# Attention in a transformer layer kernel: maxima of the first three key groups from the split keys in 32-row products, and a reordered end

## The reference, cut to what matters

```python
x = x + xattn(layernorm(x), ctx)          # 16 heads of 32, keys = values = ctx (4 x 2048 x 512)
    scores = einsum('bthd,bshd->bhts', q * s, k * s); w = softmax(scores); out = (w @ v) @ w_proj.T + b_proj
x = x + gated_scan_block(layernorm(x))    # rmsnorm, W_in -> u, z, g; tanh, sigmoid; scan over 128 tokens; W_out
x = x + moe(layernorm(x))                 # 8 experts of 512, top 2, and a shared expert of width 1024
```

## Time and profile before

| what | value |
|---|---|
| median of 3 runs | 531.94 us (531.33 to 532.11) |
| profiled execution, its own time | 533.81 us |
| its span | 532.0 us |
| PE busy | 472.7 us (89%) |
| DVE busy | 404.4 us (76%) |
| ACT busy | 327.2 us (61%) |
| POOL busy | 290.3 us (55%) |
| chain that ended last | PE 51%, DVE 27%, issue 8%, DMA 7%, ACT 3%, POOL 2% |

### The profile page before, as it was taken

The page is one execution under the profiler, slowest core; times in us unless marked ns, Lnnn a source line. Parts: engine busy times, 40 slices in busy tenths (PEclk is TensorE's granted clock), DMA queues, the critical chain, the costliest instruction groups (busy, mean ns, idle before and its releaser), DMA issues.

```text
span 532.0 us, 15785 instructions
## 1 busy us (share of the span) xinstructions
PE 472.7 (89%) x6731; PEld 330.7 (62%) x6731; DVE 404.4 (76%) x598; ACT 327.2 (61%) x362; POOL 290.3 (55%) x274
## 2 busy tenths in 40 slices
PE   0568888999999999999989945999999999999994
PEld 0135655676667767767666533844878788787642
DVE  3567576778877888787762798698599999999426
ACT  3336466766766787676654473456579888888320
POOL 1146499899999999999769430482001101010032
PEclk9999798999999999999999996999999999999998
DMA  6885789988899987897991830086999999997125
GB/s 203 243 225 170 188 228 269 241 240 236 240 254 266 262 257 208 222 261 185 362 403 56 297 121 37 1 270 220 420 358 419 417 418 417 416 417 328 41 80 177
DMA packets 29821, 133.97 MB, mean 252 GB/s; under 512 B 6452, under 2 KB 6708, under 8 KB 18996
## 3 DMA queue, kind: packets, MB, share of 16 engines
q1 hardware_dynamic: 25880, 120.38, 69.2%
q0 software_dynamic: 3680, 12.06, 6.2%
q10 hardware_dynamic: 192, 0.52, 0.5%
HBM read 96.77 MB, written 11.01 MB: 203 GB/s over the span
## 4 chain that ended last, share of the span: by engine, by line
PE 51%; DVE 27%; issue 8%; DMA 7%; ACT 3%; POOL 2%; SPq 1%; DVEq 0%; ACTq 0%; POOLq 0%
PE bank L1026 10%; PE bank L1061 10%; DVE ws L807 9%; PE bank L1046 8%; DVE mx L722 7%; PE bank L1070 6%; DMA wst<-in_ffw 5%; PE bank L1186 2%; PE bank L1187 2%; PE bank L1188 2%; DVE hf L948 1%; PE bank L1129 1%; POOL ps L638 1%; DVE hl L953 1%; DMA kstk<-kl 1%
## 5 line engine op out<-in xcount | busy, mean ns | idle before, releaser
L722 DVE TENSOR_REDUCE mx<-bank 128x1 f32<-128x512 f32 x240 | 154.7, 686 | 56.7 <-PE bank L1026 54.7
L638 POOL TENSOR_TENSOR ps<-pt 128x512 f32<-128x512 f32 x128 | 159.6, 1273 | 13.2 <-PE bank L1070 6.7
L477 ACT ACTIVATE pt<-bank 128x1024 f32<-128x1024 f32 x128 | 124.3, 1023 | 63.6 <-PE bank L1046 62.3
L807 DVE SCALAR_TENSOR_TENSOR ws<-wst,ws 128x2048 f16<-128x2048 f32 x51 | 115.5, 2283 | 1.8 <-ACT ws L525 1.2
L525 ACT ACTIVATE ws<-wst 128x2048 f16<-128x2048 f32 x48 | 90.7, 1905 | 6.1 <-DMA wst<-in_ffw 6.0
L613 POOL TENSOR_TENSOR kl<-kt,kh 128x512 f16<-128x512 f32 x58 | 67.6, 1186 | 27.3 <-ACT kh L442 27.2
L1201 PE MATMUL bank<-xt,ws 128*128 128x128 f16 x480 | 81.2, 219 | 0.5 <-DVE hf L948 0.5
L1202 PE MATMUL bank<-xt,ws 128*128 128x128 f16 x480 | 81.2, 219 | 0.0
L1203 PE MATMUL bank<-xt,ws 128*128 128x128 f16 x480 | 81.2, 219 | 0.0
L1026 PE MATMUL bank<-kstk,q 96*128 96x512 f16 x176 | 69.8, 423 | 10.2 <-DMA kstk<-kl 5.7
L679 POOL DMA_DIRECT2D ys_rows<-xn x15 | 8.2, 544 | 120.9 <-ACT xn L594 120.9
(11 more groups left out here) (170 smaller groups left out, 722.2 us busy)
## 6 DMA issues: line engine op xcount, KB each, us to landing
wst<-in_ffw SPq DMA_DIRECT2D x51, 1024.0 KB, 11.4
kt<-in_keysT SPq DMA_DIRECT2D x16, 1024.0 KB, 6.0
v<-in_vals SPq DMA_DIRECT2D x16, 1024.0 KB, 9.9
kstk<-kh SPq DMA_DIRECT2D x84, 128.0 KB, 4.0
kstk<-kl SPq DMA_DIRECT2D x44, 128.0 KB, 3.3
wst<-kh SPq DMA_DIRECT2D x40, 128.0 KB, 4.3
xs_rows<-biases SPq DMA_DIRECT2D x15, 256.0 KB, 3.0
x_tok<-xs_rows POOLq DMA_DIRECT2D x15, 256.0 KB, 7.9
```

The lines of the kernel that those rows point to most:

```text
L477: act.activation(pt[:, n % 4, :, :, :].rearrange("p j a t -> p (j a t)"), bank[:, 2 * (n % 2):2 * (n % 2) + 2, :].rearrange("p j n -> p (j ...
L638: pool.tensor_tensor(ps2[:, n % 4, :, :], pt[:, n % 4, 0, :, :], pt[:, n % 4, 1, :, :], ALU.add)\
L722: dve.tensor_reduce(mx[:, a, q:q + 1], bank[:, 4 + k % 2, :], AX.X, ALU.max).then_inc(m_taken, 1)
L807: dve.scalar_tensor_tensor(ws[:, home_of(q), 1, m, :, :].rearrange("p c n -> p (c n)"), wst[:, q % 2, m, :, :].rearrange("p c n -> p (c n) ...
```

## The change

- Groups 0, 1 and 2 (`ROWS = 3`) take their maxima without the stack. The queries are repeated over the four 32-row lanes and split into high and low (`zw`: ACT, then DVE for group 0 and POOL for 1 and 2), transposed by PE into `q0`, and `max_pair(j, k)` forms two blocks at a time, each as three accumulating matmuls of 32 rows by 512 columns (high by `kh`, low by `kh`, high by `kl`), the two blocks on neighbouring lanes and neighbouring banks. For groups 1 and 2 a pair waits until both banks are read.
- The start is reordered: the first norm and its queries before the key split, keys of group 1 loaded at once, the ones rows and three quarters of `x` later, the stack of group 0 behind. Statistics of batches 1 to 3 move from the start into body 1, with ACT's square root there.
- At the end, the constants load one body earlier, the first expert weights in bodies 13 and 14, POOL adds the bias in bodies 13 and 14, DVE takes the pair sums of the last group, `scale_win`, the small constants and `split_low(0, 0)` move into or right behind body 15. The residual sum `x1 + normed(x1)` becomes one DVE operation with row factors, so POOL has one addition a batch there, not two.

The diff, cut to its core:

```diff
+ROWS = 3
+    wide = wproj.bitcast(F16).rearrange("p n (a z c) -> p n a z c", a=HG, z=2)
+    zw, q0 = wide[:, 0:2, :, :, :], wide[:, 2:4, :, :, :]
...
@@ sync queue, start
+        load_k(1)
+        stack(0, 0)
+        load_k(2)
+        load_v(0)
...
-        sp.wait_ge(kt_in[0], 16)
-        sp.dma_start(x[:, 1:B, :], t["x"][:, 1:B, :]).then_inc(x_in, 16)
-        sp.wait_ge(split_hi, 2)
-        copies(0, 0, kh, (0, 2 * HD))
...
+        stack(0, 1)
         stack(1, 0)
-        load_k(2)
         stack(1, 1)
         load_k(3)
         load_v(1)
+        sp.dma_start(x[:, 1:B, :], t["x"][:, 1:B, :]).then_inc(x_in, 16)
...
+            if i == G - 4:
+                for dst, name in CONSTS:
+                    sp.dma_start(dst, t[name]).then_inc(consts, 16)
+            if i in (G - 3, G - 2):
+                for m in ((0,), (1, 2))[i - G + 3]:
+                    sp.dma_start(wst[:, 0, m, :, :], t["ffw"][0, m]).then_inc(w_in[0][m], 16)
@@ scalar
+        def wide_high(j):
+            q, _ = queries_of(j)
...
+            act.activation(zw[:, j % 2, :, 0, :].rearrange("p a (r d) -> p a r d", r=HG),
+                           q.unsqueeze(2).broadcast_to([P, HG, HG, HD]), ACT.Copy).then_inc(wide_hi, 1)
+        def take_wide(j):
...
+            for half in range(2):
+                act.activation(q0[:, j % 2, 2 * half:2 * half + 2, :, :].rearrange("k a z t -> k (a z t)"),
...
+        root(ln1_var, 1, 0, 1)
+        wide_high(0)
         for h in range(2):
             split_keys(0, h)
-        root(ln1_var, 1, 0, 1)
-        act.wait_ge(split_hi, 2)
-        stack_rows(act, 0, 1, kh, (0, 2 * HD))
...
+                if i == G - 2 and p == 1:
+                    split_first(0)
...
+                if i == 1 and p == 2:
+                    root(ln1_var, B, 1, B)
...
+        act.activation(r1[:, 0, 0:2], eps[:, :], ACT.Sigmoid)
@@ gpsimd
-        for i in range(G):
+        for i in range(G - 1):
             for hs in range(HS):
                 pair_sum(HS * i + hs)
...
+                if i in (G - 3, G - 2) and hs in (2, 5):
+                    add_bias(2 * (i - G + 3) + hs // 3)
-        add_bias()
...
         for b in range(B):
-            pool.wait_ge(h_done, b + 1)
-            pool.wait_ge(x1b_done, b + 1)
-            pool.tensor_tensor(x2[:, b, :], x2[:, b, :], xn[:, b, :], ALU.add).then_inc(x2p_done, 1)
+            pool.wait_ge(x1h_done, b + 1)
+            pool.tensor_tensor(x2[:, b, :], x2[:, b, :], bout[:, :], ALU.add).then_inc(x2p_done, 1)
@@ vector
+                if i == G - 1:
+                    for n in (HS * i + 2 * p, HS * i + 2 * p + 1):
+                        pair_sum(n)
...
+                if i == 1 and p < 3:
+                    dve.wait_ge(x_in, 16)
+                    first_norm(p + 1, p + 2)
...
+                if i == G - 1 and p == 0:
+                    scale_win()
+                if i == G - 1 and p == 1:
+                    make_constants()
...
+        split_low(0, 0)
...
+            dve.tensor_scalar(x2[:, b, :], x1[:, b, :], r1[:, 2, b:b + 1], r1[:, 1, b:b + 1], ALU.mult, ALU.add)\
+                .then_inc(x1h_done, 1)
-        dve.wait_ge(one_set, 2)
-        dve.tensor_scalar(starts[:, :], iota[:, :], float(P), None, ALU.mult)
...
-        split_low(0, 0)
@@ tensor
+        def max_pair(j, k):
+            a, q = block_of(k)
+            pe.wait_ge(wq_done, 2 * j + a // 2 + 1)
+            pe.wait_ge(split_hi, 2 * j + a // 2 + 1)
             if j > 0:
-                pe.wait_ge(m_taken, MB * j + k - 1)
-            elif k >= 6 and k % 2 == 0:
+                pe.wait_ge(m_taken, MB * j + k)
+            elif k >= 6:
                 pe.wait_ge(m_taken, k - 4)
...
+            home = 4 if j > 0 else k % 6
+            for n, (z, keys) in enumerate(((0, kh), (1, kh), (0, kl))):
...
+                for d in range(2):
+                    lanes = slice((q + d) * HD, (q + d + 1) * HD)
+                    mm = pe.matmul(bank[:, home + d, :], q0[lanes, j % 2, a, z, :], keys[lanes, j % 2, a, :],
+                                   start=(n == 0), stop=(n == 2))
...
         def first_products(i, p):
             tenants = maxima_in(i, p)
+            if tenants and tenants[0][0] < ROWS:
+                max_pair(*tenants[0])
+                for n in scores_in(i, p):
+                    scores(n)
+                if p == 1:
+                    queries(i + 2)
+                max_pair(*tenants[2])
+                return
```

More of the change, by code:

```diff
@@ L639, in pair_sum, with add_bias @@
                 .then_inc(add_done, 1)
[L641 removed]
+        def add_bias(b):
             pool.wait_ge(xn_done, B)
             pool.wait_ge(consts, NC)
[L644 to L647 removed]
+            pool.tensor_tensor(x[:, b, :], x[:, b, :], bproj[:, :], ALU.add).then_inc(xb_done, 1)
+        for i in range(G - 1):
             for hs in range(HS):
@@ L1076, in _ @@
         queries(0)
-        queries(1)
-        for k in range(MB):
-            max_scores(0, k)
+        for k in range(0, MB, 2):
+            if k == 8:
+                queries(1)
+            max_pair(0, k)
         shifted(0)
@@ L1111, in _ @@
             tenants = maxima_in(i, 3)
+            if tenants and tenants[0][0] < ROWS:
+                max_pair(*tenants[0])
+                second_products(i, 3)
+                for n in scores_in(i, 3):
+                    scores(n)
+                max_pair(*tenants[2])
+                continue
             for j, k in tenants[0:2]:
```

230 lines of the change are left out of this document (141 added, 89 removed).

## The result

The changed kernel took 536.27 us (median of 22 runs, 533.10 to 540.12), the kernel before 532.23 us (22 runs). The ratio is 1.0072, with a 95% interval of 1.0052 to 1.0092: slower, by 4.0 us, where 16.5 us less had been forecast. The profiled execution had a span of 534.1 us, 2.1 us more than before; it is the one that is taken apart here.

A forecast was written before the change was run, and what follows sets the result against it. Bounds seen: late first maxima, slow bodies 0 to 2, and POOL and DVE work ahead of `bb`. DMA-limited 12 us plus 4.5 us at the end made 16.5 us, giving 515.5 us by the median; range 508 to 526 us.

The forecast's parts named there:

- The head: Start of the kernel: first pair at about 10.6 us, 9.4 us earlier; transposes at 30.90 us move to about 24.5 us.
- the drain: Tiling mode changes around 32-row pairs: taken as 0.07 us each; at about 0.17 us, bodies 0 and 1 grow by 3 us.
- Bodies 0 and 1: Bodies holding the pairs of groups 1 and 2: forecast to take 18.5 us and 19 us.
- To 15.1 us I add: Body 0 costed from a 15.1 us body: 1.7 us products, 1.1 us shape changes, 0.6 us wait for both banks, giving 18.5 us.
- The rival that ended slower: 32-row products one after another, at the lower clock level through bodies 0 and 1: 43 us more, about 558 us; chance 0.06.
- The pairs' common wait: Bodies 0 and 1: waiting for both banks, two reductions under two `scores`, adds 0.6 us to a body.
- The root and the ones: Body 1's square root with table changes shows perhaps 0.5 us; the ones rows, issued about 10 us before `scores(0)`, are hidden.
- body 2: Third attention body, with its products on stacks ready in time: 15.5 us.
- DMA allows less: Up to `shifted(3)`: of the 15.4 us gained there, the DMA engines allow about 12 us, ends 7 and 16 us.
- The budget: Bodies 0 to 2 together: 53 us for 62.1 us, 9.1 us saved.
- The end: After attention: `bb` starts at 311.9 instead of 316.38 us, 4.5 us gained, bounds 3 to 5 us.
- the chain from `bb` on: From the scan's `bb` onward: the chain and the experts keep their lengths, their order not touched.

The follow-up runs named there:

- e9: Changed kernel with each pair's six 32-row products in groups 1 and 2 replaced by three of 128 rows (wrong maxima); 530.47 us, ratio 0.9943 to the kernel before.
- e4: Changed kernel with `ROWS = 1`: only group 0 in 32-row products, groups 1 and 2 from their stacks again; 531.38 us, ratio 0.9975 to the kernel before.
- e8: Changed kernel plus products that nothing reads in PE's waits between scan and router; 535.20 us, ratio 1.0041 to the kernel before.
- e13: e9 with two passes for a pair's first block, one for the second, each block waiting for its own bank only; 522.65 us, ratio 0.9799 to the kernel before.
- e14: e13 plus body 1's square root replaced by a copy and the ones rows loaded at their old place (wrong results); 520.20 us, ratio 0.9756 to the kernel before.
- e1: Kernel before, its attention kept up to the last body, with only the change's end; 529.42 us, ratio 0.9938 to the kernel before.
- e7: Changed kernel plus eleven 128-row products that nothing reads in PE's waits from 21.6 us on, one wait left empty; 539.93 us, ratio 1.0092 to the kernel before.
- e3: Changed kernel with groups 1 and 2 formed block by block, each block waiting for its own bank only; 537.60 us, ratio 1.0104 to the kernel before.
- e15: e11 plus fourteen more products that nothing reads ahead of the wait for group 2's stack; 527.24 us, ratio 0.9868 to the kernel before.
- e11: e1 plus products that nothing reads in the waits between scan and router; 528.66 us, ratio 0.9908 to the kernel before.

## Why the prediction was wrong

**The head: right.** First pair forecast at 10.6 us, measured 10.39; `shifted(0)` 24.5 and 23.92; side by side, as taken from the earlier trace rows. At the higher pace it is 0.75 us from a pair's first product to the next `scores` (48.67 to 49.42 us), and three passes of 0.215 us are 0.65; in e9, with 128 rows, it is 0.65 us (38.63 to 39.28 us). The 0.10 us left are what a change of the array's shape and back costs here, where the forecast had 0.14. So the drain that the Trainium skill ("TensorEngine Tiling (Array Packing)", Key Properties) speaks of is small here, and wasn't the trouble.

**Bodies 0 and 1: the step that failed**, forecast 18.5 and 19 us, measured 29.8 and 22.6. The sentence "To 15.1 us I add" starts from a body at the higher pace. The kernel before took 20.2 us for body 0, mostly at the lower one, and I took the rise as given by the kind of work. It isn't. e4 has products of 96 rows and a body 0 that begins at the same time as the changed kernel's, and its rise is at 41.4 us. With 32 rows in their place it is at 48.7 us (57.9 in e8), and with 128 rows at 36.6 us (e9). That is 6.2 us of busy time in body 0, shown by e9. The forecast put this term at nothing. The rival that ended slower had the lower pace through bodies 0 and 1, but hung it on products one after another. They ran side by side, and the lower pace lasted through most of body 0 only, so its price of 43 us was far off. That the kernel came out slower doesn't bear that rival out.

**The pairs' common wait**, 0.6 us a body in the forecast, is 3.4 us in body 0 of e9 (6.9 to 3.5 us idle by e13, where VectorE also gets its first block sooner), and with the dips of the clock behind it 6.8 us over three bodies. The forecast put one pair of reductions under two `scores`; but three of body 0's pairs stand in a row ahead of it, with nothing between, at 1.29 us of maxima each, and the other stages have no slack left at this pace. In the changed kernel part of it was hidden by the slow products.

**The root and the ones**, taken as 0.5 us and as hidden, are together 3.8 us in the profile (60.0 to 56.2 us in bodies 0 to 2, e13 to e14), 2.3 us by the ratios, whose intervals overlap. The root delays ACT's split of group 4's keys, and behind it POOL, in whose order the queries of group 4 stand last: body 2, forecast 15.5 us, is 20.1 us. The ones were issued at 15.0 us and landed at 26.4 us; "issued about 10 us before" was right, but the DMA engines were full (a share of 0.98 from 14 to 26 us).

**DMA allows less: it never came to that.** In the changed kernel nothing came near the 12 us. With all four terms removed `shifted(3)` is 12.9 us earlier than before, just past them: the share is near its limit in body 0 (0.99), but 0.82 and 0.84 in the two bodies after it. So 12 us was no firm bound.

**The budget** of bodies 0 to 2: forecast 53, measured 72.5 us. 5.7 us go with 32 rows (e9), 6.8 with the common wait (e13), 3.8 with root and ones (e14); 3.2 us stay unexplained, most of them in body 2, where even e14 needs 17.4 for 15.5 us. These are differences of single executions taken one after another, and the same three bodies took 79.7 us in e8, so each share is rough. The ratios give 6.9, 7.7 and 2.3 us.

**The end: right by mechanism, short by size.** `bb` 4.5 us closer forecast, 3.75 us measured (3.6 in e1, 4.5 in e4). That "the chain from `bb` on" keeps its length held in seven of the eleven profiled executions with this end. In the other four, the changed kernel's among them, it was 2 us longer by the clock, which rose at 333.8 us before and at 338.8 us after. e8 gives them back. Whether the new end makes the late rise more frequent isn't settled: e1's gain of 3.3 us by the ratio leaves little room for it.

What isn't shown: why products of 32 rows go with a later rise, whether it is their rows, their number or the change of shape around them, and why e7's full 18 us at work were granted 0.50. Whether e14's gain can be had with true maxima wasn't tried; e3 gave up the common wait with true maxima and gained nothing by its ratio.

## What to carry to other kernels

Before costing a stage, read from durations of equal products which of the two paces PE runs at there, and price the stage as it stands, not as a later one does; products over few rows that save a wait can keep the whole stream at the lower pace. When two short works are paired behind one wait for two buffers, cost the pair as a chain of both engines, and check it at the higher pace, where nothing hides it. A wait of PE costs more than its length when the clock falls behind it: where the engine has to wait anyway, products that nothing reads were worth 2.1 us ahead of a stack (profile and ratio) and 1.6 to 1.8 us by the ratios between scan and router. Ahead of body 0 they gained nothing by the ratio, with one wait left empty. Before a lost stretch is put down to a change, look at the same code in every other trace: the 2.1 us behind `bb` came and went with no edit there.

## What the runs showed of the hardware

- Three passes of a pair over 32 rows, side by side on neighbouring lanes, take 1.28 us at the lower pace and 0.65 us at the higher, plus 0.10 us for going in and out of this shape (0.75 us from 48.67 us). They overlap also when the second block's products are issued behind all of the first's (e3, 36.50 to 37.97 us).
- With three passes over 128 rows instead (e9) the pace doubled for the rest of body 0 at 36.6 us and not at 48.7 us; busy PE time of the body fell from 24.2 to 18.0 us.
- The granted clock read 1.00 from 24 to 48 us while 512 columns took 0.43 us, and 0.50 from 36 to 54 us in e7 at the same pace. At the start only the durations tell the level.
- Filler in a wait of 3.63 us kept the clock at 1.00 in the body behind it (e15; 0.84 without, e11). With filler in the waits from 21.6 us on (e7) the higher pace came at 25 us, and behind an empty wait of 1.45 us it was gone at 32.06 us.
- The same code between scan and router had its clock back 17 to 19 us after `bb` in seven profiled executions and some 23 us after it in four, worth 2 us.
